# Packing the adjacency bits with the packing matrix as the stationary operand and a VectorE transpose behind it

## The reference, cut to what matters

```
Wh = h @ W                                            # 8192 x 128
e  = leaky_relu((Wh @ a1)[:, None] + (Wh @ a2)[None, :])
att = softmax(where(adj > 0, e, -big), axis=1)        # 8192 x 8192
x  = x + act(att @ Wh)                                # act: none, elu, elu(h + .) with a threshold on att, elu
```

## Time and profile before

| | |
|---|---|
| profiled execution | 3869.88 us, of which 3868.1 us are the span of the trace |
| PE, DVE, ACT busy over the span | 99%, 92%, 32% |
| layer 0 (about 60 to 1040 us), a stretch of 240 us in it | PE 240.0, DVE 212.4, ACT 177.6 us busy, DMA share 0.88 |
| PE's clock | 1.00 of full speed in that stretch |

### The profile page before, as it was taken

The page is one execution under the profiler, slowest core; times in us unless marked ns, Lnnn a source line. Parts: engine busy times, 40 slices in busy tenths (PEclk is TensorE's granted clock), DMA queues, the critical chain, the costliest instruction groups (busy, mean ns, idle before and its releaser), DMA issues.

```text
span 3868.1 us, 83711 instructions
## 1 busy us (share of the span) xinstructions
PE 3812.6 (99%) x35490; PEld 3803.6 (98%) x35490; DVE 3568.6 (92%) x7788; ACT 1223.6 (32%) x2547; POOL 17.0 (0%) x107
## 2 busy tenths in 40 slices
PE   7999999999999999999999999999997999999999
PEld 6999999999999999999999999999997999999999
DVE  7988989888899999999999999999997999999998
ACT  6777777777631111111133121121121000000000
POOL 1000000000000000000000000000000000000000
PEclk9999999999999999999999999999998999999999
DMA  7888888888400200000002000000000000000000
GB/s 237 297 293 291 294 289 293 287 290 293 145 18 20 18 20 20 18 20 20 15 15 67 17 20 20 18 20 20 18 18 13 17 12 18 15 15 15 15 18 9
DMA packets 223271, 344.10 MB, mean 89 GB/s; under 512 B 72496, under 2 KB 147632, under 8 KB 222896
## 3 DMA queue, kind: packets, MB, share of 16 engines
q1 hardware_dynamic: 221168, 338.48, 27.9%
q10 hardware_dynamic: 1728, 0.27, 0.0%
HBM read 305.70 MB, written 21.20 MB: 85 GB/s over the span
## 4 chain that ended last, share of the span: by engine, by line
PE 96%; ACT 2%; DVE 1%; DMA 0%; issue 0%; DVEq 0%; SPq 0%; ACTq 0%; POOL 0%
PE acc L1251 93%; PE ps_pack L1165 1%; PE ps_wh L1269 1%; ACT vals L1446 1%; ACT adj_pairs L1354 0%; DMA vals<-in_x_dram 0%; DVE q L787 0%; PE acc L1233 0%; PE ps_bc L1209 0%; DVE mask L760 0%; DMA adj_int<-in_adj_dram 0%; PE acc L1188 0%; ACT xnew L1458 0%; ACT e L1374 0%; ACT wh L1380 0%
## 5 line engine op out<-in xcount | busy, mean ns | idle before, releaser
L1251 PE MATMUL acc<-vals,q 128*128 128x129 f32 (+1 forms) x32576 | 3669.1, 275 | 4.8 <-DVE q L787 4.8
L1251 PEld LDWEIGHTS acc<-vals,q 128*128 128x128 f32 x32576 | 3652.4, 192 | 6.5 <-issue 5.1
L787 DVE SCALAR_TENSOR_TENSOR q<-rrow,R,mask 128x512 f32<-128x512 f32 x3968 | 2827.0, 747 | 164.9 <-PE acc L1251 20.9
L1354 ACT ACTIVATE adj_pairs<-adj_int,threshold 128x1024 uint8<-128x1024 int32 x512 | 585.3, 1145 | 221.6 <-PE ps_pack L1165 149.0
L760 DVE TENSOR_SCALAR mask<-bits 128x512 uint16<-128x512 uint16 x2048 | 437.0, 288 | 7.4 <-DMA rrow<-rows 4.3
L1458 ACT ACTIVATE xnew<-acc,rec 128x128 f32<-128x128 f32 x244 | 69.2, 366 | 855.9 <-DVE rec L825 760.9
L1465 ACT ACTIVATE e<-xnew 128x512 f32<-128x512 f32 x47 | 29.7, 631 | 405.7 <-DVE xnew L856 317.3
L1478 ACT ACTIVATE e<-xnew,nm,rs 128x128 f32<-128x128 f32 x193 | 79.6, 482 | 218.5 <-DVE nm L632 218.5
L1531 ACT ACTIVATE wh<-ps_wh 128x512 f32<-128x512 f32 x48 | 28.7, 598 | 336.8 <-PE ps_wh L1269 335.9
L1473 ACT ACTIVATE sd<-ve 128x4 f32<-128x4 f32 (+1 forms) x49 | 9.9, 202 | 365.5 <-DVE ve L613 365.5
L856 DVE SCALAR_TENSOR_TENSOR xnew<-mean,none,xnew 128x128 f32<-128x128 f32 x188 | 65.1, 346 | 51.8 <-ACT xnew L1458 51.8
(11 more groups left out here) (229 smaller groups left out, 729.3 us busy)
## 6 DMA issues: line engine op xcount, KB each, us to landing
adj_int<-in_adj_dram SPq DMA_DIRECT2D x512, 512.0 KB, 5.0
rrow<-rows SPq DMA_DIRECT2D x60, 256.0 KB, 3.3
x_between_layers<-xnew SPq DMA_DIRECT2D x32, 256.0 KB, 4.2
xin<-x_between_layers SPq DMA_DIRECT2D x32, 256.0 KB, 2.8
xin<-in_x_dram SPq DMA_DIRECT2D x16, 256.0 KB, 5.4
wh_of_layer<-wh SPq DMA_DIRECT2D x1, 4096.0 KB, 16.8
x_of_layer<-xnew SPq DMA_DIRECT2D x16, 256.0 KB, 2.3
xin<-x_of_layer SPq DMA_DIRECT2D x16, 256.0 KB, 2.8
```

What stands on the lines that cost most here:

```text
L787: nc.vector.scalar_tensor_tensor(q[:, j % RING, :], row, column(R_, t), mask[:, c % 2, j, :], ALU.max, ALU.mult).then_inc(q_ready, 1)
L1251: last = nc.tensor.matmul(to, q[:, j % RING, b * P:(b + 1) * P], vals[:, t, 0:width(g.layer)], start=first, stop=(t == KT - 1 or g.two and ...
L1354: nc.scalar.activation(adj_bytes[:, n % BIN_RING // 2, :, n % 2], adj_int[:, n % ADJ_RING, :], ACT.Sign, bias=threshold[:, 0:1], accum_out ...
```

## The change

Of the 64 chunks, those from number 6 on (`FIRST_TURNED`), 58 in all, are packed the other way round. The first six (the first ones are made while layer 0 starts) stay as they are.

```diff
+FIRST_TURNED = 6
+TURN_AT = 12
+        turned_words = adj_pairs[:, BIN_RING // 2 - 1, 0:JC * WORDS].bitcast(U16)
+        words_copied = sem("words_copied")
+        words_turned = sem("words_turned")
@@ VectorE: unpack, turn_words, between
                 if g.layer == 0:
-                    dve.wait_ge(bits_ready, g.value * CHUNKS + (c + 1))
+                    C = g.value * CHUNKS + c
+                    if C < FIRST_TURNED:
+                        dve.wait_ge(bits_ready, C + 1)
+                    else:
+                        dve.wait_ge(words_turned, C + 1 - FIRST_TURNED)
+            def turn_words(C):
+                v, c = C // CHUNKS, C % CHUNKS
+                dve.wait_ge(words_copied, C + 1 - FIRST_TURNED)
+                nc.vector.transpose(bits[:, v, c * JC:(c + 1) * JC, :].rearrange("p t w -> p (t w)"), turned_words)\
+                    .then_inc(words_turned, 1)
+                    if g.layer == 0 and t % JC == TURN_AT:
+                        C = g.value * CHUNKS + t // JC + 1
+                        if FIRST_TURNED <= C < CHUNKS * GROUPS:
+                            turn_words(C)
@@ TensorE: pack
-                need(pe, bits_ready, v * CHUNKS + c)
+                C = v * CHUNKS + c
+                need(pe, bits_ready, min(C, FIRST_TURNED))
+                need(pe, words_copied, C - FIRST_TURNED)
                 for i in range(0, QP, 2):
                     pe.wait_ge(adj_binary, v * PIECES + (c * QP + i + 2))
+                    if C >= FIRST_TURNED:
+                        pairs = adj_pairs[:, i // 2, :].rearrange("p (t b j) -> p b t j", t=PT, b=BLOCKS)
+                        half = i // BLOCKS
+                        for b in range(BLOCKS):
+                            last = nc.tensor.matmul(ps_pack[b * WORDS:(b + 1) * WORDS, half * 256:(half + 1) * 256],
+                                                    packer[:, i % BLOCKS // 2, :], pairs[:, b, :, :],
+                                                    start=(i % BLOCKS == 0), stop=(i % BLOCKS == 2), skip_group_check=True)
+                        last.then_inc(adj_packed, 2)
+                        continue
@@ ScalarE: binary, words
+                if n % BIN_RING == BIN_RING - 2:
+                    need(act, words_turned, v * CHUNKS + n // QP - FIRST_TURNED)
+                if v * CHUNKS + c >= FIRST_TURNED:
+                    nc.scalar.activation(turned_words, ps_pack[:, :], ACT.Copy, scale=2.0 ** 24).then_inc(words_copied, 1)
+                    return
```

## The result

The changed kernel took 3863.55 us (median of 19 runs, 3862.18 to 3865.3), the kernel before 3870.74 us beside it (19 runs): a ratio of 0.9982, 95% interval 0.9976 to 0.9989. That is 7.2 us less, in the direction forecast, but under half of the 17.4 us that were forecast. The profiled executions differ by 6.5 us in their span.

What follows compares the result with a forecast made beforehand. Layer 0 was taken as bounded by PE: 58 packs of 0.81 us go (47.0), 58 of 0.51 come (29.6), so 3869.88 - 47.0 + 29.6 = 3852.5, plus 0.3 for the median: 3852.8 us. Range 3845 to 3886 us, likeliest case 3848 to 3859.

Steps and rivals of the forecast that it cites:

- a round of four: In a pack, a slot's four matmuls go to four column groups and stream together, costing one stream of 0.105 us.
- rival 4: In every pack, column groups don't stream together: pack 1.77 us, +56 us, 3926 us, slower; chance 0.15.
- ACT's wait of 1.2 us in the second chunk: At piece 6, ACT waits 1.2 us for DVE's transpose; its 3.49 us stand before the next pack swallows it.
- seams: Weight loads exposed at a pack's two ends: 0.03 us at the start plus 0.06 at the end, 0.09 us.
- the forecast 0.30 us a pack: PE's saving per pack: 0.51 us forecast for the new pack against 0.81 us for the old, over 58 packs.
- rival 2: DVE gives the gain back; PE stands about 0.6 us at tile 32 in 14.5 sweeps: +9, 3862 us; chance 0.08.
- a pack takes 0.45 to 0.6 us from its first start to the next tile's: A sign in PE's timeline that would show the forecast right.
- Rival 3: Each mode switch empties the array: pack 1.03 us, +13 us, 3883 us, slower; chance 0.09 together with rival 5.
- what the prediction counts as the same: Whole-kernel times indistinguishable from no change, about 0.2% or 7.7 us: 3862.5 to 3877.9 us; chance 0.14.
- Rival 1: Loads between the matmuls, or the seams, fill PE: pack 0.73 us, -5 us, 3865 us; chance 0.08.
- The case of 0.62 us: A pack with groups together at the skill page's efficiency, 2.38 of 3: 0.62 us, gain 11 us.
- rows 6: Trace rows where a 64-column matmul between full ones starts on pace, the next 0.11 us later; read as nothing emptied.

Runs made afterwards that it cites:

- the transposes alone: Kernel before, PE's packing untouched, plus 56 VectorE transposes at tile 12 and ScalarE's wait for them at piece 6: 3870.75 us, ratio 1.0000.
- the kernel without ACT's wait: Changed kernel with raw words copied into the next chunk's place in bits, and ScalarE's wait for the transpose at piece 6 removed: 3862.77 us, ratio 0.9982.
- the probes: Kernel before with extra unread matmuls or transposes of several widths and types after chunks' last tiles in layer 3, two kernels: 3892.28 and 3890.86 us.
- doubled visits: Changed kernel with each of the 58 turned packs cut in two, two slots after tile 7 and two after tile 15: 3880.28 us, ratio 1.0025.
- a paired visit: Two chunks packed per PE visit, on the changed kernel without ScalarE's wait at piece 6; three versions: 3862.33, 3865.07 and 3858.77 us.

## Why the prediction was wrong, step by step

**What held.** That layer 0 is PE's, that a round of four costs one stream of about 0.105 us (0.110; rival 4 is out), the 0.60 us of the transpose (0.62), ACT's wait of 1.2 us in the second chunk (1.15) and that it is swallowed (the transposes alone: ratio 1.0000), the direction.

**The step that failed** is the seams: "I take 0.03 + 0.06 = 0.09 us". They are 0.308 us: 0.093 going in where the sum has 0.03, 0.010 in the first round, and 0.205 coming out, in two steps of 0.10, where the sum has one of 0.06. In pieces, against the forecast 0.30 us a pack: seams 0.218 more, rounds 0.018 more, and the old pack 0.076 dearer than I had it (0.886, since I counted to the next tile's first start and put the late second one into the tiles' pace). That leaves 0.30 - 0.218 - 0.018 + 0.076 = 0.14 us; 58 x 0.14 = 8.1 us. PE's waits for `q` at the packs take 0.8 us of that (1.3 now, 0.5 before; two of the four are at tile 32, where rival 2 put them, and the kernel without ACT's wait mostly lacks them). The longer wait at the layer's end takes another 0.9 us, for which the prediction has no term. 6.4 us are left, against 6.5 us between the two spans. The dearer old pack was luck: it gave back 0.076 x 58 = 4.4 us.

**What the signs missed.** "... a pack takes 0.45 to 0.6 us from its first start to the next tile's" came true (0.55) though the forecast failed: this count leaves out the gap ahead of the pack and the late second tile matmul behind it. Rival 3's sign, a gap of 0.2 us at either side, was there, read from start to start (0.205 and 0.202), and pack to pack was 15.04 us and not 14.9. The measured 3863.55 us also lies in what the prediction counts as the same (3862.5 to 3877.9), to which it gave 0.14, though the interval of the ratio excludes no change. Rival 1 (chance 0.08) had the nearest number, a pack of 0.73 us and 3865, but got it mostly from loads between the matmuls, and those hide: rounds stay at 0.109 us. The case of 0.62 us, in which four groups together run at less than full speed, is out too.

**Why it failed.** I had rival 3's mechanism, and set it aside on one row: "a matmul with 64 stationary columns stands between full ones ... Nothing was emptied". That row is a transpose, `nc.tensor.transpose` at L1214, and the probes show that a transpose of that shape has no gap and a matmul of that shape has. The row said nothing about the case. The shape in a row isn't the whole form of an instruction. The line in the code was there to be read.

The rule that I weighed against this row fits what the runs show: the Trainium skill's "TensorEngine Tiling (Array Packing)", Key Properties, has a change of tiling mode drain TensorE. The trace agrees, with +0.093 us going in, +0.205 us coming out, where the tile's load is no longer issued ahead, and 0.159 us between widths. The same page, Gotcha 2 (feature incompatibilities), says that column tiling and transpose mode on f32 input exclude each other; the transposes without a gap agree with that, and it would have told me that rows 6 was no test. Only rival 3's price was too high, 0.61 us against 0.308: it has a latency and a load each way, 0.259 going in and 0.355 coming out, and the trace shows 0.103 (with the first round) and 0.205.

That the gap lies in the visit and not in DVE or ACT is shown from three sides: doubled visits cost 0.29 us each, a paired visit is 0.31 us shorter than two, and DVE's part alone costs nothing. What happens inside TensorE in these 0.093 us is not shown.

## What to carry to other kernels

Narrow matmuls in separate column groups do run together, but price the visit, not the stream: here it cost 0.31 us for going in and coming out, so that a saving of half the streaming time came down to a sixth of the pack's cost. Put as much as possible into one visit, and see that what is moved to make room stands where its engine was idle anyway. When one row is to rule out a mechanism, look up in the code what instruction it is.

## What the runs showed of the hardware

- Four float16 matmuls in the four groups of 32 columns start about 3 ns apart; a round of 256 columns takes 0.11 us. With 128 columns, four rounds over the four groups cost 0.532 us and four matmuls in a single group 0.522 us.
- Going from full-width matmuls to a group of 32 or 64 columns costs 0.093 us over the pace of 0.112, float16 or f32; weight loads are not issued ahead across the change. Coming back from a stream of 256 columns, the next two f32 matmuls start after 0.202 and 0.214 us. From a group of 32 to one of 64 the next start comes after 0.159 us, as it does to full width, where it is 3 ns between groups of 32. f32 transposes with 32 or 64 output rows start after 0.112 us, with their load ahead.
- Even between full-width matmuls, the second f32 matmul behind a stretch of float16 ones came 0.193 us after the first in place of 0.112 (0.166 behind a single one).
- A transpose of 128 x 512 uint16 in 32 x 32 blocks has a record of 0.70 us and holds VectorE 0.62 us.
